# A four-layer gated network on one core: the last layer's experts computed over rows sorted by expert, in place of every expert for every batch

## What is computed

```
x = x + tanh(g_xattn[3]) * perceiver_attention(ctx, layernorm(x), ...)
xn = layernorm(x)                                    # 2048 rows of 128
scores = softmax(xn @ gate_w.T)                      # 8 experts
top_scores, sel = top_k(scores, 2)                   # two experts for each row
x = x + tanh(g_ffn[3]) * sum over the two chosen e of
        score_e * (silu(xn @ w1[e]) * (xn @ w3[e])) @ w2[e]    # hidden width 256
```

## Time and profile before

| | us |
|---|---|
| median of three runs | 1395.59 |
| span of the profiled execution (its total time is not given) | 1388.9 |
| TensorE busy | 1236.4 |
| VectorE busy | 820.1 |
| ScalarE busy | 640.5 |
| GpSimd busy | 575.0 |
| first matmul of the last layer's experts | 1206.5 |
| start of the final store | 1383.4 |

### The profile page before, as it was taken

The page is one execution under the profiler, slowest core; times in us unless marked ns, Lnnn a source line. Parts: engine busy times, 40 slices in busy tenths (PEclk is TensorE's granted clock), DMA queues, the critical chain, the costliest instruction groups (busy, mean ns, idle before and its releaser), DMA issues.

```text
span 1388.9 us, 26338 instructions
## 1 busy us (share of the span) xinstructions
PE 1236.4 (89%) x9595; PEld 859.2 (62%) x9595; DVE 820.1 (59%) x2600; ACT 640.5 (46%) x1310; POOL 575.0 (41%) x1098
## 2 busy tenths in 40 slices
PE   6999655799999969999799989988989899999997
PEld 3444222367778734554688834444777567799997
DVE  5788486555454357884566678873555543355654
ACT  1677553355554336675222227765223365343341
POOL 4443272866763385630433544433233585100000
PEclk9999856999999968999899959998999999999999
DMA  4000000000000040000000000001200000000001
GB/s 135 11 1 2 1 1 0 1 1 1 1 1 1 1 134 3 2 2 1 2 0 0 1 0 2 2 2 24 112 1 1 1 1 1 1 1 0 0 0 31
DMA packets 15336, 16.84 MB, mean 12 GB/s; under 512 B 6403, under 2 KB 12565, under 8 KB 14583
## 3 DMA queue, kind: packets, MB, share of 16 engines
q1 hardware_dynamic: 15222, 15.34, 3.6%
HBM read 14.28 MB, written 1.05 MB: 11 GB/s over the span
## 4 chain that ended last, share of the span: by engine, by line
PE 38%; POOL 5%; DVE 5%; issue 3%; ACT 1%; DVEq 0%; POOLq 0%; ACTq 0%
PE banks L3094 7%; PE banks L2455 4%; PE banks L3105 4%; PE banks L2203 3%; PE banks L2481 2%; PE banks L2819 2%; PE banks L2193 2%; PE banks L519 1%; PE banks L2790 1%; PE banks L558 1%; PE banks L2804 1%; PE banks L2866 1%; DVE x_resident L2146 1%; PE banks L2464 1%; PE banks L753 1%
## 5 line engine op out<-in xcount | busy, mean ns | idle before, releaser
L533 DVE TENSOR_REDUCE x_minus_max<-banks 128x2 f32<-128x512 f32 x256 | 169.9, 687 | 53.5 <-PE banks L519 52.2
L541 ACT ACTIVATE x_probs<-banks 128x512 f32<-128x512 f32 x256 | 151.7, 600 | 87.0 <-PE banks L525 85.8
L519 PE MATMUL banks<-x_kT,x_qT 32*128 32x256 bf16 x512 | 103.6, 303 | 19.6 <-DVE x_minus_max L533 10.7
L3094 PE MATMUL banks<-xnT,w_f_w 128*128 128x256 f32 x512 | 120.8, 379 | 0.0
L525 PE MATMUL banks<-x_qT,x_kT 32*128 32x256 bf16 x512 | 98.0, 287 | 2.4 <-ACT x_probs L541 1.7
L3094 PEld LDWEIGHTS banks<-xnT,w_f_w 128*128 128x128 f32 x512 | 92.5, 190 | 10.0
L1806 DVE CUSTOM_DVE_ANT_0 x_work<-banks,hide_later_keys 128x128 f32<-128x128 f32 (+1 forms) x256 | 80.0, 352 | 26.5 <-PE banks L1919 24.9
L3065 ACT ACTIVATE f_gate<-banks 128x512 f32<-128x512 f32 x64 | 38.2, 597 | 110.2 <-PE banks L3094 110.2
L3028 DVE TENSOR_TENSOR f_hiddenT<-banks,f_gate 128x512 f32<-128x512 f32 x64 | 44.2, 691 | 66.2 <-PE banks L3105 50.1
L519 PEld LDWEIGHTS banks<-x_kT,x_qT 32*128 32x128 bf16 x512 | 28.5, 95 | 86.6 <-DVE x_minus_max L533 49.4
L1850 ACT ACTIVATE x_work<-banks 128x384 f32<-128x384 f32 x128 | 62.6, 495 | 42.1 <-PE banks L1925 41.5
(11 more groups left out here) (513 smaller groups left out, 3078.9 us busy)
## 6 DMA issues: line engine op xcount, KB each, us to landing
w_f_w<-in_f_w SPq DMA_DIRECT2D x5, 1024.0 KB, 6.9
out<-x_resident SPq DMA_DIRECT2D x1, 1024.0 KB, 5.1
x_resident<-in_x SPq DMA_DIRECT2D x1, 896.0 KB, 6.0
context_rows<-in_ctx SPq DMA_DIRECT2D x1, 768.0 KB, 4.8
contextT<-in_ctxT SPq DMA_DIRECT2D x1, 672.0 KB, 8.2
w_f_wg<-in_f_wg SPq DMA_DIRECT2D x1, 544.0 KB, 4.8
w_f_wu<-in_f_wu SPq DMA_DIRECT2D x1, 544.0 KB, 5.8
w_f_wd<-in_f_wd SPq DMA_DIRECT2D x1, 512.0 KB, 6.2
```

What stands on the lines that cost most here:

```text
L519: mm = nc.tensor.matmul(K.PS[:, SMAX0 + m % 2, t * S:(t + 1) * S], h["qT"][r, c % 3, g, t * P:(t + 1) * P], h["kT"][r, c % 3, g, :], start ...
L533: K.nc.vector.tensor_reduce(h["nm"][:, b % 2, :, n], K.PS[:, SMAX0 + n % 2, :].rearrange("p (t n) -> p t n", t=T), AX_X, ALU.max, negate=T ...
L541: K.nc.scalar.activation(h["p"][:, n % (2 * HG)], K.PS[:, ST0 + n % 2, :], ACT.Exp).then_inc(s["p"].sem, 1)
L3094: mm = nc.tensor.matmul(K.PS[:, 2 * (e % 2) + k, c * S:(c + 1) * S], W[name][:, e * HE3 + c * P:e * HE3 + (c + 1) * P], K.norm["xnT"][:, u ...
```

## The change

Each row is now written twice to a region in DRAM, once for each of its two experts, at a place sorted by expert: expert e owns the rows from 2048 e on, and a running count over all batches gives the place inside. A row there has 130 words: 128 values, its weight, and the row of the result it belongs to (its home). GpSimd writes with indirect DMAs, 128 rows each, four for a batch. The gating of the eight batches runs in eight stages, placed in 36 slots alongside the last slots of x3. Then VectorE makes a table that gives the expert and the place of each of 23 tiles of 256 rows (4096 rows are at most 16 full tiles and 7 partly filled ones; the tile count is fixed). For each tile SP loads the expert's weights (384 KB, three slots in turn) and the 256 rows (130 KB, four slots in turn), at addresses read from the table; TensorE transposes the rows and does `up` and `down`, VectorE multiplies by the weight, and GpSimd writes the rows to their homes in a second DRAM tensor with two indirect DMAs. At the end SP loads both results of each row back, VectorE adds them to x, and SP stores x batch by batch. SP clears the region with ten DMAs after the first layers' loads. The weights of the last layer's experts are no longer loaded ahead. Some semaphores of other layers get another name.

```diff
+ROW3 = D + 2
+CHUNKS3 = B * S // S
+ROWS3 = (NE3 * CHUNKS3 + 1) * S
+TILES3 = B * S * K3 // S + NE3 - 1
+NOWHERE = 1 << 20
+ROW_SLOTS, WEIGHT_SLOTS = 4, 3
+SORT_SLOTS, SCATTERED3 = 3, 16 * T * K3
+GATES3 = (5, 9, 12, 15, 18, 21, 24, 28)
+GATE_STAGES3 = 8
+X3_QUERIES_AT = 10
...
+def gated(slot, stage):
+    return [b for b in range(B) if GATES3[b] + stage == slot]
...
+    def sync(sp):
+        chunks = region.rearrange("(c t p) d -> c p t d", t=T, p=P)
+        experts = K.dram["f3_w"].rearrange("(e p) n -> e p n", p=P)
+        sp.wait_ge(table.sem, table.after(0))
+        def fetch_weights(j):
+            i = j % WEIGHT_SLOTS
+            e = sp.value_load(t["table"][0:1, 1, j:j + 1], min_val=0, max_val=NE3 - 1)
+            if j >= WEIGHT_SLOTS:
+                sp.wait_ge(tile["down"].sem, tile["down"].after(0, j - WEIGHT_SLOTS + 1))
+            sp.dma_start(t["w"][i], experts[bass.ds(e, 1)].rearrange("e p n -> p (e n)")).then_inc(weights_in[i].sem, 16)
+        def fetch_rows(j):
+            i = j % ROW_SLOTS
+            c = sp.value_load(t["table"][0:1, 0, j:j + 1], min_val=0, max_val=NE3 * CHUNKS3)
+            if j >= ROW_SLOTS:
+                sp.wait_ge(sent[i].sem, sent[i].after(0, 16 * T * (j // ROW_SLOTS)))
+            sp.dma_start(t["in"][:, i], chunks[bass.ds(c, 1)].rearrange("c p t d -> p (c t) d")).then_inc(row_in[i].sem, 16)
+        fetch_weights(0)
+        fetch_weights(1)
+        for i in range(SORT_SLOTS):
+            sp.wait_ge(scattered[i].sem, scattered[i].after(0))
+        fetch_rows(0)
+        fetch_rows(1)
+        for j in range(2, TILES3):
+            fetch_weights(j)
+            fetch_rows(j)
+        for i in range(ROW_SLOTS):
+            sp.wait_ge(sent[i].sem, sent[i].after(0))
+        homes = result.rearrange("(k n p) d -> p k n d", k=K3, p=P)
+        for b in range(B):
+            for k in range(K3):
+                sp.dma_start(t["back"][k][:, b].rearrange("p (n d) -> p n d", d=D), homes[:, k, b * T:(b + 1) * T]).then_inc(back_in[b].sem, 16)
+        for b in range(B):
+            sp.wait_ge(s["done"].sem, s["done"].after(b))
+            sp.dma_start(K.out.rearrange("(n p) d -> p n d", p=P)[:, b * T:(b + 1) * T], K.X[:, b * S:(b + 1) * S].rearrange("p (n d) -> p n d", d=D)) \
+                .then_inc(stored.sem, 16)
+        sp.wait_ge(stored.sem, stored.after(0))
...
+        def normal_rows(b):
+            u = b % 2
+            dve.wait_ge(s["rstd"].sem, s["rstd"].after(b))
+            i = b % SORT_SLOTS
+            if b >= SORT_SLOTS:
+                dve.wait_ge(scattered[i].sem, scattered[i].after(0, b // SORT_SLOTS * SCATTERED3))
+            for k in range(T):
+                nc.vector.tensor_scalar(t["rows"][:, i, k, :, 0:D], K.X[:, b * S + k * P:b * S + (k + 1) * P].unsqueeze(1).broadcast_to([P, K3, D]),
+                                        n["mv"][:, u, k, 0:1], n["rs"][:, u, k:k + 1], ALU.subtract, ALU.mult).then_inc(s["rows"].sem, 1)
...
+        def place(b):
+            u = b % 2
+            uv, parts, sums = t["uv"], t["parts"], t["sums"]
+            rank = K.PS[:, MISC + 1, 2 * T * NE3:3 * T * NE3].rearrange("p (t e) -> p t e", t=T)
+            dve.wait_ge(s["rank"].sem, s["rank"].after(b))
+            nc.vector.tensor_tensor(t["at"][:], rank, t["first"][:].unsqueeze(1).broadcast_to([P, T, NE3]), ALU.add).then_inc(s["ranked"].sem, 1)
+            dve.wait_ge(s["ranked"].sem, s["ranked"].after(b))
+            step(nc.vector.tensor_tensor(uv[:, :, 0], t["at"][:], t["sel"][:, u], ALU.mult))
+            step(nc.vector.tensor_reduce(t["high"][:], uv[:, :, 0], AX_X, ALU.max))
+            step(nc.vector.tensor_tensor(t["last"][:], uv[:, :, 0], t["high"][:].unsqueeze(2).broadcast_to([P, T, NE3]), ALU.is_ge))
+            step(nc.vector.tensor_tensor(parts[:, 1], uv[:], t["last"][:].unsqueeze(2).broadcast_to([P, T, 2, NE3]), ALU.mult))
+            step(nc.vector.tensor_tensor(parts[:, 0], uv[:], parts[:, 1], ALU.subtract))
+            step(nc.vector.tensor_reduce(sums[:], parts[:], AX_X, ALU.add))
+            nc.vector.tensor_copy(t["rows"][:, b % SORT_SLOTS, :, :, D], sums[:, :, :, 1].rearrange("p k t -> p t k")).then_inc(s["placed"].sem, 1)
+            nc.vector.tensor_copy(t["at_row"][:, b % SORT_SLOTS], sums[:, :, :, 0].rearrange("p k t -> p t k")).then_inc(s["placed"].sem, 1)
...
+        def hidden(j):
+            dve.wait_ge(tile["g"].sem, tile["g"].after(0, j + 1))
+            nc.vector.tensor_tensor(t["hT"][j % 2], K.PS[:, 2 * (j % 2) + 1, :], t["g"][j % 2], ALU.mult) \
+                .then_inc(tile["h"].sem, 1)
+        def weighted(j):
+            i = j % ROW_SLOTS
+            dve.wait_ge(tile["down"].sem, tile["down"].after(0, j + 1))
+            if j >= ROW_SLOTS:
+                dve.wait_ge(sent[i].sem, sent[i].after(0, 16 * T * (j // ROW_SLOTS)))
+            for k in range(T):
+                ins = nc.vector.tensor_scalar(t["out"][:, i, k], K.PS[:, OUT0 + j % 2, k * D:(k + 1) * D], t["in"][:, i, k, D:D + 1], None, ALU.mult)
+            ins.then_inc(tile["y"].sem, 1)
...
+        for slot in range(GATES3[-1] + GATE_STAGES3):
+            for b in gated(slot, 0):
+                row_stats(b)
+            for b in gated(slot, 1):
+                normal_rows(b)
+            for b in gated(slot, 7):
+                place(b)
+            for b in gated(slot, 3):
+                biggest(b)
+            for b in gated(slot, 4):
+                scores(b)
+            for b in gated(slot, 5):
+                choose(b)
+            yield
+        tile_table()
+        for j in range(TILES3):
+            hidden(j)
+            if j:
+                weighted(j - 1)
+        weighted(TILES3 - 1)
+        for b in range(B):
+            x = K.X[:, b * S:(b + 1) * S]
+            dve.wait_ge(back_in[b].sem, back_in[b].after(0, 16 * K3))
+            step(nc.vector.tensor_tensor(x, x, t["back"][0][:, b], ALU.add))
+            nc.vector.tensor_tensor(x, x, t["back"][1][:, b], ALU.add).then_inc(s["done"].sem, 1)
...
+        def scatter(b):
+            i = b % SORT_SLOTS
+            pool.wait_ge(s["ids"].sem, s["ids"].after(b))
+            pool.wait_ge(s["placed"].sem, s["placed"].after(b))
+            for k in range(T):
+                for which in range(K3):
+                    nc.gpsimd.indirect_dma_start(region, bass.IndirectOffsetOnAxis(t["at_row"][:, i, k, which:which + 1], 0), t["rows"][:, i, k, which], None) \
+                        .then_inc(scattered[i].sem, 16)
...
+        for j in range(TILES3):
+            i = j % ROW_SLOTS
+            pool.wait_ge(tile["y"].sem, tile["y"].after(0, j + 1))
+            for k in range(T):
+                nc.gpsimd.indirect_dma_start(result, bass.IndirectOffsetOnAxis(t["in"][:, i, k, D + 1:D + 2].bitcast(U32), 0), t["out"][:, i, k], None,
+                                             bounds_check=K3 * B * S - 1, oob_is_err=False).then_inc(sent[i].sem, 16)
...
+        def turned(j):
+            act.wait_ge(tile["turned"].sem, tile["turned"].after(0, j + 1))
+            nc.scalar.activation(t["inT"][j % 2], K.PS[:, MISC + j % 2, 0:S], ACT.Copy).then_inc(tile["inT"].sem, 1)
+        turned(0)
+        turned(1)
+        for j in range(TILES3):
+            act.wait_ge(tile["up"].sem, tile["up"].after(0, j + 1))
+            nc.scalar.activation(t["g"][j % 2], K.PS[:, 2 * (j % 2), :], ACT.Silu).then_inc(tile["g"].sem, 1)
+            if j + 2 < TILES3:
+                turned(j + 2)
...
+        def turn(j):
+            i = j % ROW_SLOTS
+            pe.wait_ge(row_in[i].sem, row_in[i].after(0, 16 * (j // ROW_SLOTS + 1)))
+            if j >= 2:
+                pe.wait_ge(tile["inT"].sem, tile["inT"].after(0, j - 1))
+            for k in range(T):
+                mm = nc.tensor.transpose(K.PS[:, MISC + j % 2, k * P:(k + 1) * P], t["in"][:, i, k, 0:D], K.ident[:])
+            mm.then_inc(tile["turned"].sem, 1)
+        def up(j):
+            i = j % WEIGHT_SLOTS
+            pe.wait_ge(weights_in[i].sem, weights_in[i].after(0, 16 * (j // WEIGHT_SLOTS + 1)))
+            pe.wait_ge(tile["inT"].sem, tile["inT"].after(0, j + 1))
+            if j >= 2:
+                pe.wait_ge(tile["h"].sem, tile["h"].after(0, j - 1))
+            for k in range(2):
+                for c in range(CE3):
+                    mm = nc.tensor.matmul(K.PS[:, 2 * (j % 2) + k, c * S:(c + 1) * S], t["w"][i][:, k * HE3 + c * P:k * HE3 + (c + 1) * P], t["inT"][j % 2],
+                                          start=True, stop=True)
+            mm.then_inc(tile["up"].sem, 1)
+        def down(j):
+            i = j % WEIGHT_SLOTS
+            pe.wait_ge(tile["h"].sem, tile["h"].after(0, j + 1))
+            if j >= 2:
+                pe.wait_ge(tile["y"].sem, tile["y"].after(0, j - 1))
+            for k in range(T):
+                for c in range(CE3):
```

(36 more changed lines are left out.)

383 lines of the change are left out of this document (208 added, 175 removed).

## The result

The changed kernel takes 1499.73 us (median of four runs, 1495.0 to 1507.59) against 1394.21 (four runs of the kernel before): ratio 1.0775, 95% interval [1.0732, 1.0818]. That is slower, as forecast, but 105 us slower, not 46: the time is 59 us over the forecast and 18 over the range. The profiled execution has a span of 1493.0 us and is the one of 1495.0, so here 2.0 us lie around the span. (The 6.7 us that the prediction put around the span of the kernel before are mostly scatter between its executions: where both numbers are known for one of them, they lie 1.8 to 1.9 us apart.) The chip has a second, slower state, which three runs fell into that the ratios leave out: one of four with six weight slots (1453.69) and two of four in the experiment called Both.

What follows compares the result with a forecast made beforehand. The prediction took the experts to be bound by TensorE alone. Rows ready at 1252, 162 us of tile loop and a 20.5 us tail gave 1434.5, 45.6 over the 1388.9 span, so about 1441 us; range 1372 to 1482.

Steps and rivals of the forecast that it cites:

- What bounds the kernel before: Last layer's experts: bound by TensorE alone, 64 steps of 2.62 us, 168 of the 176 us; 23 tiles take 60.
- Placing of the last batch, 1245: Gating before the tiles: VectorE binds with 62 us of gating, 11 of attention and 7 of waits from 1165.
- The period of a tile, 7.5: Tile loop: 2.88 us of TensorE work, 3.3 exposed by SP's order of waits, 1.3 for the clock.
- second rival: Tile loop: the clock stays low, period 9.1 us, time 1477; chance 10%.
- Other loops are looser: Tile loop: a row slot returns 5.7 us after down(j-4) and is wanted at 7.1, so it does not bind.
- The tail, 20.5: After the last down: weighting, indirect DMAs, landing, 16 loads, additions and store sum to 19.5 to 21.5 us.
- rival 3: Tile loop and scatter: POOL binds if one indirect DMA takes above 3.7 us; time 1463, chance 8%.
- At no cost: Outside the last layer: clearing 8.7 MB of DRAM, dropped weight loads, semaphore renames and ScalarE's table switches change no time.
- The rule of the Trainium skill: Gating: scatters beside a later batch's normal rows would wait some tenths of a us each; left out of the sum.
- The clock that stays up (1): Tile loop: idle times of 3.3 us don't lower the clock, period 6.2 us, time 1415; chance 16%.
- Rival 5: Tile loop: bound by TensorE, row loads land behind other work, tiles every 2.9 us, time 1347; chance 14%.
- rival 4: Before the tiles: gatings hide under attention, rows ready at 1228 instead of 1252, time 1417; chance 8%.

Runs made afterwards that it cites:

- Both: Changed kernel with rows asked for before weights and 12 unused products ahead of each wait for rows: 1417.48 and 1424.59 us in the two runs that count.
- the loosened kernel: Changed kernel with rows asked for before weights, six weight slots, seven slots for rows and results, five for scattered rows: 1367.99 us, ratio 0.9808.
- the rows first: Changed kernel with SP asking for the rows of each tile before its weights: 1432.38 us, ratio 1.027.
- the kernel with swap and short choice: The loosened kernel with placing put before normal rows and experts chosen by one comparison, equal scores not handled: 1360.37 us, ratio 0.9782.
- the short choice: The loosened kernel with one comparison in place of eleven small operations that choose among equal scores: 1367.06 us, ratio 0.9785.
- the swap: The loosened kernel with a batch's placing before the normal rows of the batch two behind it in VectorE's queue: 1367.62 us, ratio 0.9824.

## Why the prediction was wrong

**What bounds the kernel before** was right: in the loosened kernel TensorE is bound by its own work again, at 2.84 us a tile, and 61.9 us lie between the first tile's return and the last one's, where the 64 expert steps took 176. Most of that gain pays for what now stands ahead of the loop and behind it; 25 us are left.

**Placing of the last batch, 1245.** Measured: the last sums at about 1254. VectorE was busy some 61 us from 1165 to 1254, attention's 11 included, so the gating was 50 where 62 were taken. But the waits were 28, not 7. VectorE's longest waits in this stretch, by what ended them (us in total, times, longest):

```profile
DVE x_minus_max L2630 <- PE banks L2796: 7.1, 4, 3.8
DVE f_logits L3062 <- PE banks L3276: 5.8, 4, 2.5
DVE f_rows L3056 <- DMA f_sorted_rows<-f_rows,f_scatter_rows: 3.9, 3, 1.7
```

The first is attention's own, the second the gating's logits: TensorE's queue ends more of VectorE's waiting than the scatters do. The chain of waits, though, runs from 1207 us on mostly along GpSimd and its DMAs. GpSimd's part the prediction had priced for the last batch alone; each batch holds it for 5 us of indirect DMAs, ahead of the next row scale. Taking one of these waits away gave under 3 us each time. So the size of this miss is measured, and its split among the engines is not. VectorE was busy 65% of the time from 1165 to 1240, where the sign asked for over 80%, busy or waiting in its own chain. Behind that: 0.7 us until the first scatter starts (1254.84), 4.7 for the four (4.8 forecast), and 3.0 until the last has landed (2.0). Rows ready at 1262.5, not 1252: **10.5 us**.

**The period of a tile, 7.5.** This is the step that failed. Measured 10.0 to 10.5 in fourteen of twenty, 9.7 as their mean. By its terms, in a tile of 10.1: hop and weights' issue 0.5, as forecast; from there to the rows' issue 0.76, where 0.4 was taken for the register load; landing 2.95 to 3.0, where 2.2 was taken. Together **4.3 exposed, not 3.3**. The other way of counting, with the weights ahead in the queue, had given 3.2; from the weights' issue to the rows' landing it was 4.1. The larger miss is **the clock: 2.9 us a tile over the forecast's 2.88, and 2.6 on average, not 1.3**. Of the 44 us that the twenty periods are over their 150, the clock makes some 26 and the exposed part some 18. The prediction's second rival, low level all through, had 9.1 for the period and 10% of the chance; with 4.3 for the exposed part it would have had 10.1, to the tenth. The reading behind 1.3 was that of the earlier trace rows, where groups after one idle time are stretched in part. There the idle time stood alone, with long work at full clock around it. Here an idle time of 4.3 us follows every 5.8 us of work, and the clock is down through all the work of fourteen tiles in twenty: 3.41 for L3310. The products ahead of the wait gave back 3.0 us of a tile of 10.1, with the exposed load still there, which shows that it is the clock that idle time costs, and not the transfer.

From rows ready to the last `down`: 210 us, where 162 were forecast, **48 us** and four fifths of the whole miss. Of these the twenty periods are 44, and the way to the first `down` (10.8 us, 8 forecast) 3. The start is 10.5 of the rest.

**Other loops are looser** was right for the kernel as changed, and gave the wrong margin for what came behind: the row slots bind at 6.5 us a tile, once the first wait is gone. The prediction had rows return 5.7 us after `down` and no load time behind it; in the chain with the rows first they return after 4.8, and the load adds 2.3.

**The tail, 20.5:** 20.8. The terms as written add up to 19.3, so the number was right in part by rounding up. The 1.5 us that lay between are the sixteen loads: 11.1 us from the first issue to the last landing, where 9.6 were forecast.

```profile
1476.15 2.11 DMA f_returned_rows<-f_tile_out,f_tile_rows
...
1478.41 0.38 SPq L3025
...
1485.99 3.56 DMA w_f_w<-f_returned_rows
...
1489.57 0.44 DVE x_resident L3173
```

**GpSimd's indirect DMA, 1.2:** 0.95 to 1.07 busy and 0.30 before the next, 1.27. A sound price; rival 3 is out. The Trainium skill, DMA: Bandwidth & Descriptors, "Anatomy of one DMA", has a fixed 2.0 us for such a DMA; the 2.1 us from the start to the end of the last one that returns a tile's rows agree. The last of the four that scatter a batch ends 2.3 to 2.5 us after its start, and that of the last batch 3.9.

**At no cost** is not contradicted: the mix step that stood at 1164.87 stands at 1164.83. But that is one execution against one, and this point scatters by up to 27 us between the others, so a cost of some us for clearing, renamed semaphores or the weight loads that went would not be seen.

**The rule of the Trainium skill**, SBUF — State Buffer, "SBUF: two separate sides", would have made the scatters beside normal rows wait. It speaks of VectorE operations in a mode that uses two ports, and no row tells whether the normal rows ran in one. In the kernel with swap and short choice a scatter's first indirect DMA starts at 1234.74, beside normal rows from 1234.73 to 1235.47, and takes 1.05 us; the first of batches 1 to 3, with none beside them, take 1.05 to 1.07. That is no such wait. The very first indirect DMA takes 1.26 us in every kernel, with normal rows beside it that take 0.90 to 0.93 us in place of 0.73; whether that is the two meeting or a first use isn't shown. The sum without the rule lost a few tenths of a us at most.

**The rivals.** The clock that stays up (1) had 16%, the one that stays low (2) 10%. "Long bursts in f32" spoke for the first; with bursts of 5.8 us and 4.3 us idle the clock came back within the burst in six tiles of twenty only. The measured time lies above both, since the exposed part was 1 us longer than in either. Rival 5 named the mechanism that decides for or against the change. Its 14% was for the kernel as written, where SP's order excludes it, as the text itself said. Its "under 5.3 with rival 4's early start" should read 5.1: 24 us over twenty periods add 1.2 to its 3.9.

## What to carry to other kernels

Before counting what a loop's engines must do, follow for each buffer who asks for it, behind what, and when it comes back: this change cut TensorE's work in the experts to somewhat over a third and came out 105 us slower, some 65 of them by one wait standing ahead of a request that didn't need it, and won 25 against the kernel before when requests and slots were loosened. In this loop an idle time that recurs in every round cost twice, once as itself (4.3 us) and once as work at the lower clock (2.6 us on average); a forecast with such a wait is nearer when it takes that work at the lower level throughout, unless a row shows the clock up in a loop of the same rhythm. When two waits stand one behind the other, removing one can show next to nothing, as the short choice and the swap did alone: take both away before calling either harmless. An edit that brings a landing forward gains only what the work behind it can use (2.5 us of landing, 0.7 at the end). And compare from a common event in the traces if layers ahead of the change scatter, with a second trace of the same kernel to tell how far that measure itself moves.

## What the hardware showed that I had not expected

- Rows asked for right behind 384 KB of weights land after 2.3 to 3.1 us, mostly 2.95, without weights ahead after 2.1 to 2.4, so the load ahead costs mostly 0.7, less than the 1.05 us that its bytes take at the rate of the earlier trace rows.
- Between two DMA issues of SP that take their address from memory lie 1.1 us: 0.35 for the first, 0.27 and 0.15 in the register loads, the rest in steps of 0.03 to 0.05.
- Four indirect DMAs of 128 rows follow each other every 1.27 us; the first of a batch comes 0.74 us after the wait for its addresses ends.
- The clock came back to 1.00 with products that nobody uses ahead of each wait (30 a tile: 1300 to 1400 us at 1.00; 12 a tile: 1300 to 1340 at 1.00, 1340 to 1400 at 0.91).
